# Attention's value product at full column width (32 for 17), and its output bank no longer cleared

## The reference

```python
x = x + tanh(g_xattn[0]) * xattn(layernorm(x), ctx, ctx)
x = x + tanh(g_ffn[0]) * ffn(layernorm(x), w_router, w_gate, w_up, w_down, ...)

def xattn(q, k, v):            # 8 heads; a head has 16 of the 128 rows
    qk = einsum('bdm,bdn->bmn', qh, kh) / sqrt(16)
    sm = softmax(qk, axis=-1)  # 512 x 512 for each of 128 heads
    return einsum('bmn,bcn->bcm', sm, vh)
```

## Time and profile before

| what | value |
|---|---|
| times of three runs | 1286.5, 1301.37, 1305.22 us |
| median | 1301.37 us |
| the profiled execution | 1301.37 us, its span 1299.2 us |
| PE, busy | 1186.1 us (91%) |
| DVE, busy | 767.0 us (59%) |
| ACT, busy | 517.4 us (40%) |
| POOL, busy | 569.2 us (44%) |
| mean granted clock of PE | 0.978 |

### The profile page before, as it was taken

The page is one execution under the profiler, slowest core; times in us unless marked ns, Lnnn a source line. Parts: engine busy times, 40 slices in busy tenths (PEclk is TensorE's granted clock), DMA queues, the critical chain, the costliest instruction groups (busy, mean ns, idle before and its releaser), DMA issues.

```text
span 1299.2 us, 21684 instructions
## 1 busy us (share of the span) xinstructions
PE 1186.1 (91%) x6020; PEld 774.6 (60%) x6021; DVE 767.0 (59%) x1195; ACT 517.4 (40%) x1040; POOL 569.2 (44%) x490
## 2 busy tenths in 40 slices
PE   2998888888888988999969999999999999999996
PEld 0333333333333334887758777777787877788885
DVE  5688888878888851873424343333333333337877
ACT  1477677767666772111101123333333333321110
POOL 2133434433334124235753633645546464318753
PEclk9999999989889999999979999999999999999999
DMA  9346556656555523966451525464554546413655
GB/s 234 107 135 188 173 170 189 159 147 182 155 162 155 135 67 123 397 233 234 138 195 49 194 62 181 155 208 154 173 183 152 197 158 210 152 67 114 178 162 178
DMA packets 104814, 214.57 MB, mean 165 GB/s; under 512 B 12352, under 2 KB 17472, under 8 KB 104768
## 3 DMA queue, kind: packets, MB, share of 16 engines
q1 hardware_dynamic: 85408, 152.08, 38.1%
q0 software_dynamic: 18016, 61.88, 14.5%
q10 hardware_dynamic: 1344, 0.04, 0.1%
HBM read 117.48 MB, written 91.75 MB: 161 GB/s over the span
## 4 chain that ended last, share of the span: by engine, by line
PE 57%; issue 1%; DVE 1%; another core or an unknown queue 1%; DVEq 0%; ACT 0%
PE score_ps L131 18%; PE score_ps L1491 17%; PE d_ps L1446 9%; PE d_ps L1514 8%; PE score_ps L1472 3%; PE d_ps L1503 1%; PE d_ps L1399 1%; DVE y_all L1293 1%; DVE y_all L1281 0%; DVE hid L1307 0%; DVEq L154 0%; DVE th L1301 0%; ACT th L1101 0%; PE score_ps L1408 0%
## 5 line engine op out<-in xcount | busy, mean ns | idle before, releaser
L585 DVE TENSOR_REDUCE maxima<-score_ps 128x2 f32<-128x1024 f32 x256 | 308.3, 1222 | 46.2 <-PE score_ps L690 43.5
L538 ACT ACTIVATE probs<-sb_ps 128x512 f32<-128x512 f32 x512 | 278.3, 596 | 115.0 <-PE sb_ps L704 109.2
L131 PE MATMUL score_ps<-yn_t,w_split 128*128 128x512 f32 x1056 | 256.7, 401 | 5.1 <-issue 4.3
L1491 PE MATMUL score_ps<-w_split,x_split 128*128 x948 | 236.6, 398 | 0.0
L131 PEld LDWEIGHTS score_ps<-yn_t,w_split 128*128 128x128 f32 x1056 | 201.0, 191 | 57.6 <-issue 8.0
L1491 PEld LDWEIGHTS score_ps<-w_split,x_split 128*128 128x128 f32 x948 | 172.3, 188 | 33.1
L1010 POOL CAST w_split<-w_raw 128x1024 fp32r<-128x1024 f32 x63 | 66.0, 1048 | 251.8 <-POOLq L1080 140.7
L1012 POOL TENSOR_TENSOR w_split<-w_raw,w_split 128x1024 fp32r<-128x1024 f32 x63 | 151.9, 2411 | 5.1
L715 PE MATMUL o_ps<-probs,v_t 128*17 128x512 f32 x1024 | 143.2, 633 | 0.0
L1446 PE MATMUL d_ps<-w_split,h_split 128*128 128x512 f32 x528 | 127.5, 394 | 8.9 <-issue 7.0
L1514 PE MATMUL d_ps<-w_split,h_rows 128*128 x474 | 120.3, 389 | 0.0
(11 more groups left out here) (143 smaller groups left out, 1312.0 us busy)
## 6 DMA issues: line engine op xcount, KB each, us to landing
xs_dram<-zero SPq DMA_DIRECT2D x1, 20224.0 KB, 57.5
stage<-xs_dram SPq DMA_DIRECT2D x79, 256.0 KB, 2.7
res_dram<-stage SPq DMA_DIRECT2D x79, 256.0 KB, 2.0
k_dram<-k_hi SPq DMA_DIRECT2D x16, 512.0 KB, 2.9
q_dram<-q_hi SPq DMA_DIRECT2D x16, 512.0 KB, 3.9
w_raw<-in_L_ffn_w_gate_dram POOLq DMA_DIRECT2D x16, 512.0 KB
w_raw<-in_L_ffn_w_up_dram POOLq DMA_DIRECT2D x16, 512.0 KB
w_raw<-in_L_ffn_w_down_dram POOLq DMA_DIRECT2D x16, 512.0 KB
```

The source lines that it names most:

```text
L131: mm = pe.matmul(dst[i], w[:, k, f * P:(f + 1) * P], self.yn_t[:, b, k, t * self.SPAN:(t + 1) * self.SPAN], start=(n == 0), stop=(n == 3 * ...
L538: act.activation(probs[:, c % 2, head(j)[2], :], sb_ps[:, j % 2, :], ACT.Exp, scale=SCALE).then_inc(exp_done, 1)
L585: dve.tensor_reduce(maxima[q % 2][:, :].rearrange("p (h u) -> p u h", u=8)[:, u, :], sa_ps[:, u % 2, :, :], AX_X, ALU.max).then_inc(max_do ...
L1491: mm = pe.matmul(gu_ps[j], x_split[j][:, b, k, :], w_split[:, bass.ds(at + (a * 3 * ex.PIECE + k * 2 * FE), 2 * FE)], start=(n == 0), stop ...
```

## The change

The V product takes all 32 stationary columns of a head, and writes all 32 partitions of its place in `o_ps`. The added columns of `v_t` are those that are cleared at the start and not written again. DVE's memset of `o_ps`, its semaphore and PE's wait for it are gone.

```diff
-        o_cleared = sem("o_cleared")
...
-            dve.memset(o_ps[:, :], 0.0).then_inc(o_cleared, 1)
...
-                    mm = pe.matmul(o_ps[32 * j:32 * j + HD + 1, :], v_t[q % 2][:, c, j, 0:HD + 1], probs[:, c % 2, j, :],
+                    mm = pe.matmul(o_ps[32 * j:32 * j + 32, :], v_t[q % 2][:, c, j, :], probs[:, c % 2, j, :],
                                    start=(c == 0), stop=(c == KC - 1))
...
-            pe.wait_ge(o_cleared, 1)
```

## The result

| | before | after |
|---|---|---|
| median, us | 1295.05 (20 runs) | 1302.05 (20 runs) |
| lowest to highest, us | 1286.5 to 1305.22 | 1292.27 to 1316.34 |
| profiled execution, us | 1301.37 | 1302.71 |
| its span, us | 1299.2 | 1300.6 |
| mean granted clock | 0.978 | 0.980 |

The ratio of after to before is 1.0055, with a 95% interval of 1.0033 to 1.0078. The change makes the kernel about 7 us slower (4 to 10 by the interval): within 2%, so "no change" by the bound used ahead, and inside the forecast range, but on the other side of no change from the 1291 us that was forecast. The single time the sum started from, 1301.37 us, was itself 6 us above what 20 runs of the same kernel have as their median.

The account below looks back on a forecast made before the run. Attention was taken as bound by PE and ACT passing the stage back and forth. 1301.4 + 1.7 (weights) - 0.4 (memset) - 11.8 (clock) = 1290.9 us, range 1285 to 1306, 0.95 for within 2%.

Parts of the forecast that it names:

- the rest is not argued about: nothing in it changes: Expert products after attention, some 800 us: claimed unchanged, beginning when attention ends, and set aside.
- long satisfied: 0: PE's wait for the cleared o_ps bank: claimed already met, so removing it changes the time by 0.
- the large term: Granted clock in attention: all four falls to 1.2 GHz claimed to go, -11.8 us; chance 0.47.
- the clock falls as before: Rival for attention's granted clock: all falls remain, time 1302.7 us; chance 0.42.
- The price of a fall: Attention slots: each clock fall claimed to cost 2.94 us, 2.54 in its slot and 0.40 in the one behind.
- The weights: V product's weight loads in attention: 13 ns more for one exposed load per group, 128 times, +1.7 us.
- rival with a dearer product: V product in attention: queued loads give 1314.3 us, array places running two and two 1403; chance 0.06.
- sign of being wrong on the product: Attention slots: undisturbed ones growing by more than 0.1 us would refute the product estimate.
- The clearing: DVE's o_ps memset at attention's start: its removal lets the first reduction start earlier, -0.40 us.

Follow-up runs that it names:

- places 0 and -1 to +1: PE instructions ahead of the expert tile loop, relative to before; step over the jump 5.281 to 5.283 us at -1, 5.080 to 5.086 at 0, 5.085 and 5.089 at +1.
- the wait gone alone: Before with only PE's wait for o_cleared removed, narrow product and memset kept; 1302.44 us, ratio 1.0052.
- one behind the loop: After with one more PE instruction, a long-met wait, directly behind the expert tile loop; 1301.61 us, ratio 1.0085.
- one more: After with one long-met wait for s_const added on PE ahead of its first attention slot; 1299.62 us, ratio 1.0039.
- the wide product alone: Before with the product widened to 32 columns, memset and both waits kept; 1298.8 us, ratio 1.0033.
- two more: After with three lines of the long-met s_const wait ahead of PE's first slot, code two instructions longer than after's; 1292.87 us, ratio 0.9974.
- one ahead of the loop: After with one more PE instruction, a long-met wait, directly ahead of the expert tile loop; 1290.17 us, ratio 0.9988.
- narrow with two more: Before, 17 columns and memset kept, with two more PE instructions ahead of its first slot; 1287.83 us, ratio 0.9975.

## Why the prediction was right or wrong

**The step that failed: "the rest is not argued about: nothing in it changes".** No instruction of the expert block changed, but one PE instruction ahead of it went, and the loop over tiles behind it lost 0.196 us in each of 36 jumps, 7.1 us. The prediction treated the removed wait as free because it is "long satisfied: 0". That it waits for nothing was right; that its removal is free was not. What the runs show instead is the dear jump: 331 ns for 127 between the loop's first two instructions, in the kernel with only this wait removed as well as in the whole change. The difference between the instruction ahead of and behind the loop (1290.17 and 1301.61 us, both beside the same wide product) is 11.4 us, of which the jumps are 7.1; another 2 go with the clock (23.7 and 26.4 us lost to it, as counted below), and the rest is within the 4 us that each ratio can be off.

**The clock: the large term failed, the rival "the clock falls as before" was right.** The sum took 11.8 us off for four falls that would go, and this term alone gave the forecast its direction. After's profile has 27.3 us at 1.2 GHz in attention, before's has 27.3. Taking for each run (1 - mean granted clock) x span as the clock lost, the means are 25.1 us in after (35 runs), 28.7, 29.8, 25.2, 23.7 and 26.4 in the other wide ones at places 0 and -1 to +1, against 26.9 and 24.7 in two sets of runs of before, 27.2 and 22.2 in the narrow variants. Wide and narrow lie in each other's midst. The number of falls moves by itself, from run to run, and these runs show no effect on it of the columns at work, 68 or 128. The prediction argued that a small difference might tip it, with "is shown by no row" beside it; it was a guess in the place of a term, and at 11.8 us it was larger than all other terms together.

The price of a fall was misread as well. The 0.40 us for the slot behind it (14.01 us for 13.61) is not the fall's: in the slot of 14.01 us DVE's subtraction of the maxima took 603 ns where it otherwise takes 175, which is the collision described below. Over the thirteen traces, of the slots of that parity behind a fall, 24 without such a collision took 13.57 to 13.63 us, and 31 with one 13.71 to 14.08. By the earlier trace rows a fall of 6.8 us costs the 2.54 us of its own slot, and four would have been 10.2.

The rival's sum was 1302.7, and the median is 1302.05, but that meeting is luck: the sum was made on an execution that was 6 us above the median, and 7 us in the loop made up for it.

**The weights: right in size.** Predicted: 13 ns for a group, 1.7 us in all. Measured: 12 ns (984 to 996), 128 times, 1.5 us. The load grew from 97 to 109 ns, and one load per group is exposed, as taken. The slots agree: where neither a fall nor a collision disturbs them, those of the shorter parity, in the second half of attention, took 13.56 to 13.61 us in the three narrow traces (mean 13.59, 13 slots) and 13.60 to 13.64 in the ten wide ones (mean 13.62, 25 slots), 0.03 us more for four groups. No rival with a dearer product came: no sign of queued loads or of places that no longer run side by side. As foreseen, undisturbed slots of one parity did not grow by more than that: 14.05 and 13.90 before, and after

```profile
297.49:311.56 14.07, 12.23 (x79) 4.96 (x81) 12.73 (x20) 9.58 (x19) 6.35 (x6) 1.00 0.69 205
311.56:325.62 14.06, 12.04 (x78) 4.68 (x78) 11.49 (x15) 10.09 (x21) 4.52 (x4) 1.00 0.60 142
```

The second of these is of the parity that took 13.61 before, though, and it grew by 0.45 us, far more than 4 x 0.012 and more than the 0.1 us that the prediction named as its sign of being wrong on the product. The next term is the reason for that, not the product.

**A term that was missed: DVE's subtraction meets GpSimd's cast.** Timeline of both engines and of the transpose of the maxima behind them, in that slot before:

```profile
315.04 0.17 DVE L596 TENSOR_TENSOR max_parts<-maxima,max_parts 128x16 f32<-128x16 f32 x1
...
315.05 0.64 POOL L457 CAST yn_t<-yn 128x512 f32 x1 [1.67 <-ACT yn L525]
...
315.36 0.27 PE L723 MATMUL m_ps<-ident,max_parts 128*32 128x128 f32 x1 [0.55 <-DVE max_parts L596]
```

And after:

```profile
316.24 0.61 POOL L456 CAST yn_t<-yn 128x512 f32 x1 [1.67 <-ACT yn L524]
...
316.27 0.61 DVE L595 TENSOR_TENSOR max_parts<-maxima,max_parts 128x16 f32<-128x16 f32 x1
...
317.02 0.27 PE L721 MATMUL m_ps<-ident,max_parts 128*32 128x128 f32 x1 [1.02 <-DVE max_parts L595]
```

Before, the subtraction started 10 ns ahead of the cast and took 0.17 us. After, it started 30 ns behind the cast and took 0.61, as long as the cast, and PE's transpose waited 1.02 us for 0.55. A few tens of ns in PE's stage decide which comes first. The Trainium skill (SBUF — State Buffer, SBUF: two separate sides) has this as a lock: a VectorE operation with two inputs in SBUF and a GpSimd operation that reads SBUF share a port pair, and whichever starts first holds it for its whole length. For VectorE the traces agree: in all 19 places of the two traces where the subtraction began behind the cast (by 19 to 201 ns), it ended 26 to 29 ns behind the cast's end, after 461 to 617 ns. For GpSimd they agree in part: a cast that began 7 to 13 ns behind the subtraction took about 640 ns for 611, some 30 ns more and not the 165 that the subtraction still ran; spans on GpSimd are rough, though.

How often it happens, from the lines view of 32 subtractions (busy us, mean ns, idle before), before and after:

```profile
L596 DVE TENSOR_TENSOR max_parts<-maxima,max_parts 128x16 f32<-128x16 f32 x32 | 8.6, 268 | 1.1
```

```profile
L595 DVE TENSOR_TENSOR max_parts<-maxima,max_parts 128x16 f32<-128x16 f32 x32 | 9.9, 308 | 1.1
```

1.3 us more in all; 11 of 32 took over 300 ns, before 8. The three narrow kernels have 8, 6 and 6 such, the ten wide ones 8 to 12 (9.8 in the mean). What one costs can be read from the slots: of those of the shorter parity without a fall, and the first and last few left out, 64 without a collision took 13.56 to 13.64 us and 103 with one 13.71 to 14.09, about 0.4 us more. Three more collisions are 1.3 us. That the wider product brings them is a correlation; no experiment took the collision away.

**The clearing: right.** Predicted 0.40 us earlier, measured 0.59 at the first T product, and the wait did move onto the reduction. Over more traces it is about 0.5: from the tanh to the first T product it is 14.90 to 14.99 us in the four kernels with the memset, and 14.40 to 14.54 in the seven without it that have at most 16 added instructions there.

**The sum made again.** Jumps +7.1, groups +1.5, collisions +1.3, clearing -0.5: 9.4 us. The ratio measured gives +7.0 with 4.3 to 10.1 around it. Since the clock lost differs between sets of runs, and the time rises by about 0.8 us for each us of it over all these runs, the kernels can also be put beside before at equal clock loss: after +9.9 us, the wait gone alone +7.4, one behind the loop +9.2; one more +3.7, the wide product alone +2.2, two more +0.4, one ahead of the loop -0.2, narrow with two more -1.5. The three with the dear jump stand apart by over 3.5 us from the rest. Within the rest they spread over 5 us, wide and narrow beside each other, and that is what leaves the wide product's 2.8 us (groups and collisions) unseparated in the times. One more and the wide product alone, both a few us above before, fit these 2.8; one ahead of the loop, just as wide, does not show them. This clock lost leaves out the first 45 to 65 us, which the last section comes to. Attention's length in the thirteen traces, from the first T product to the last copy of `o_sb`, can be fitted with it: 0.43 us for each us at 1.2 GHz behind those first us, 0.35 us for each us of the slow beginning, and 1.5 us (standard error 0.6) for the wide product, with 0.9 us of scatter left. This estimate is a little over half of the 2.8, and in its error's reach of them.

**Did any version beat both?** After with one instruction ahead of the loop (0.9988) and before with two more (0.9975) have intervals that hold 1. They beat after, and cannot be told from before.

## What to carry to other kernels

Taking out an instruction that costs nothing can cost time far behind it: where a loop follows on the same engine, compare its steps in both traces, the step over the jump back apart from the others, and look at "issue" idle time there and at the sequencer's records; when only it grew, move the loop by one harmless instruction before looking for a cause in the data. A part of the program that the diff doesn't touch is not a part whose time is known. And a term that rests on "may well tip it" belongs among the rivals with its chance, not into the sum, above all when the kernel's own repeats move by more than it.

## What the hardware showed that was not expected

- The same loop of PE takes 0.196 us more per jump back at one place of its code than at six others, the next one among them. Nothing waits for a semaphore there: the idle time is "issue" (0.17 us at the good places, 0.36 to 0.37 at the bad one), and it lies between the loop's first instruction and its second (127 and 331 ns). Lengths of 8, 16, 32 and 64 instructions are no period of it. Why is open.
- The row of granted clock does not cover the very start. Its first 9s say full speed, yet before's products took as long there as in the falls to 1.2 GHz:

```profile
L715 PE MATMUL o_ps<-probs,v_t x32: 1034/1048/1061, 43.0 to 57.8; 128*17 128x512 f32 x32
```

  (before, 43 to 58 us), where those of after from 46.6 us on took half as long:

```profile
L713 PE MATMUL o_ps<-probs,v_t x28: 592/617/617, 46.6 to 56.0; 128*32 128x512 f32 x28
```

  The trace's record of the clock begins at 64.9 us in before and at 45.8 us in after, and in all thirteen traces at 45.1 to 64.9 us. Every V product that ended ahead of that point took 1034 ns or more, and every one that started behind it and ahead of 70 us took 617 or less. So the slow beginning differs by up to 20 us from run to run, in narrow kernels (45.2, 54.9, 64.9) as in wide ones (45.1 to 64.3), and nothing ties it to the change. Up to the 150th record of PE after gained 6.4 us on before by this. That is more than the 4.8 us by which attention ended earlier in after's profile, which read alone would have looked like a gain of the change.
